# Recurrence of a two-layer kernel: one run of 128x64 score products for both inner steps, TensorE's program without its loop, and the outputs' turn placed behind the states' turns

## The chip, the cores and the metric

One core of a Trainium2 chip runs the whole program. The metric is the device time of one execution in microseconds. The kernel before takes 2533.22 us (median of 3 runs, 2533.12 to 2538.01).

## What is computed

Two adaLN layers over 16 sequences of 512 tokens with 256 channels. The attention of layer 0 is a recurrence with 16 heads of 16 dimensions: its state is two small matrices per head (4 x 16 each), updated chunk by chunk (16 tokens). Cut to what matters here:

```python
def attn(q, k, v):
    s = jnp.einsum('bqhd,bkhd->bhqk', q, k) / jnp.sqrt(jnp.asarray(q.shape[-1], q.dtype))
    p = jax.nn.softmax(s, axis=-1)
    return jnp.einsum('bhqk,bkhd->bqhd', p, v)

def step(carry, xs):
    W_in, W_out = carry
    q_t, k_t, v_t, lr_t = xs
    k_h = jax.nn.softmax(jnp.einsum('blhd,bDhd->blhD', k_t, W_in), axis=-1) * lr_t[..., 1:]
    q_h = jax.nn.softmax(jnp.einsum('blhd,bDhd->blhD', q_t, W_in), axis=-1)
    qk = jnp.einsum('bqhD,bkhD->bhqk', q_h, k_h) * mask
    o_t = jnp.einsum('bqhD,bDhd->bqhd', q_h, W_out) + jnp.einsum('bhqk,bkhd->bqhd', qk, v_t)
    W_out = W_out + jnp.einsum('bnhD,bnhd->bDhd', k_h, v_t)
    for _ in range(2):
        g_out = -attn(W_in, k_t, v_t)
        g_in = -attn(W_out, v_t, k_t)
        W_in = W_in - lr_in * g_in
        W_out = W_out - lr_out * g_out
    return ((W_in, W_out), o_t)
```

The change touches `attn(W_out, v_t, k_t)` of the two inner steps: its scores, W_out on the values of the chunk, are the "scores on the values" below.

## The kernel before

The program has three stages: projections of all 16 sequences (to about 480 us in the profile), the recurrence (481 to 1209 us), and the rest of layer 0 with layer 1 (to the end). Only the recurrence is touched.

The recurrence walks 32 chunks in order. All 16 x 16 pairs of sequence and head are done together: a state is a 128x128 tile, and for the products it lies "spread" in a 128x1024 tile, 32 blocks of 32 columns, block-diagonal by heads. The spread (`spread`, L1289 and L1848) multiplies by 0 or 1: VectorE writes the lower 64 partitions with one instruction (L1852), ScalarE the upper 64 with four (L1292). Each engine has its own program, written in the order in which it is to run; the engines meet through counting semaphores (`Steps`: `mark` raises one, `at(c, name)` is its value when step `name` of chunk c is done, `before` that of the chunk before). All five programs walk the chunks as `Fori(0, ROUNDS)` (4 rounds) around 8 chunks written out (`CPR`). As the chunk number then hangs on a register, a wait needs a register instruction ahead of it.

TensorE's order in one chunk (L871 to L944):

1. `scores` (L830) on keys and queries, marks a0 and a1, then turns of them (L884, L887, L893), and the running sums (`sums`, L846) and state terms (`add_state`, L854) of the outputs.
2. Three runs of `updates` (L841) on pb_1, pb_2, pb_kh: 32 products each (steps p1v, p2v, khv). khv closes W_out: VectorE then adds it (L1939, "wok") and the inner step's update (L1941, "wo1").
3. `turn_out` (L861, "ot"), four transposes of the normalised outputs of the chunk before, which ScalarE evicts (L1298, "oev").
4. The states' turns: transposes of w_out_k (L911, "two") and w_out_1 (L913, "tw1"), each then spread by VectorE and ScalarE ("xo", "xw").
5. `sums(3)`, then the scores on the values: two runs of 32 products of 128 rows x 32 columns x 16 tokens (L834), "b0" on st_out1 after "xo", "b1" on st_out2 after "xw".
6. Softmax of each in turn: VectorE takes the maxima (L1954) and subtracts them (L1956), ScalarE takes exp (L1360, "eb0", "eb1"), TensorE turns it (L925, L928), both spread it ("xb0", "xb1"), and between these stands half of `add_state((2, 3), ..)`.
7. `updates` on the keys (L841, "pb0"), the other half of `add_state((2, 3), ..)`, `updates` "pb1", then the turns of the new W_in (L937 "ti1", L942 "ti"), whose spreads start the next chunk.

```python
mm = pe.matmul(dst[j * NST:(j + 1) * NST, x], by_tile(st)[:, j, x], tok[:, j, x], start=True, stop=True)
```

On VectorE the order after "bs1" is: osum (row sums of the outputs, L1865), xb0, omean (L1869), xb1. GpSimd's "oc" (L1570) waits for omean.

Of the kernel before, what the change touches and what calls it, by code (L numbers as in the profile page):

```python
# [6 lines left out]
P = 128  # L7
# [13 lines left out]
ROUNDS = CHUNKS // CPR  # L21
# [51 lines left out]
def adaln_two_layers(nc, x, w_in, taps, w_out, ln_g, ln_b, w_in_init, w_out_init, u1, v1, b1, u2, v2, b2,  # L73
                     cond, wmod, w_attn, w_proj, w_r, w_k, w_v, mu, ident_c, blocks_c, parity_c, mask_c, four_c, scan_c, out):
    ctx = ExitStack()
    with ctx:
# [95 lines left out]
        st_in1, st_in2, st_out1, st_out2 = (carve(TILES * NST) for _ in range(4))  # L172
# [19 lines left out]
        m_b, rl_i = carve(2, GG), carve(2, PP)  # L192
# [60 lines left out]
        def hold(eng):  # L253
# [43 lines left out]
            "bm0", "bs0", "bm1", "bs1", "osum", "xb0", "omean", "xb1", "irec0", "ilr0", "imul0", "wi1", "irec1", "ilr1", "imul1", "wi", "xs", "xi"])  # L297
# [3 lines left out]
                                       "eb0", "eb1", "xb0", "xb1", "rv3", "rv2", "xs", "xi"])  # L301
        re_pe = Steps(sem("re_pe"), ["a0", "a1", "traw", "te1", "te2", "r01", "p1v", "p2v", "khv", "ot", "two", "tw1", "sm3", "b0", "b1",
                                     "tb0", "tb1", "pb0", "r23", "pb1", "ti1", "ti"])
# [405 lines left out]
        def _(pe):  # L709
# [126 lines left out]

            def updates(dst, pb, rows, js):

                for x in range(PP):
                    for j in js:  # L840
                        mm = pe.matmul(dst[j * NST:(j + 1) * NST, x], by_tile(pb)[:, j, x], rows[:, j * PP + x], start=True, stop=True)  # L841
                return mm
# [71 lines left out]

# [1325 lines left out]
```

## Time and profile before

| | |
|---|---|
| median of 3 runs | 2533.22 us |
| the profiled execution, its own time | 2533.14 us |
| its span | 2531.3 us |
| recurrence, 32 chunks | 481 to 1209 us, 22.75 us each |
| busy over the span | TensorE 86%, VectorE 63%, ScalarE 62%, GpSimd 43% |
| granted TensorE clock, whole span | 0.93 |

Times in the profile are microseconds from the start of the span; a line number is that of the listing above. "PE" is TensorE's matmuls, "PEld" its weight loads, DVE VectorE, ACT ScalarE, POOL GpSimd. "idle before ... <- X" tells what ended the idle time; "issue" means that nothing which the profile shows was waited for.

### The profile page before, as it was taken

To read this page: it belongs to the slowest core of one execution; us is meant where nothing else is said; L and a number is where in the kernel's file an instruction comes from. 1 tells how busy PE (TensorE), PEld (TensorE's weight loads), DVE (VectorE), ACT (ScalarE), POOL (GpSimd) and SP (SyncE) were. 2 spreads that over 40 slices of the span, in tenths; PEclk is the share of its full clock that TensorE was granted. 3 is DMA by queue.
4 is the path that set the end of the run, shared out by engine and by line. 5 is a ranking of instruction groups with operands and counts; after the bars stand their busy time and mean duration, and the time that the engine had idled before them with its cause. 6 is when DMAs were issued, how large, how long until landed. Compare 5 with 4: busy or idle time off the path is not lost.

```text
span 2531.3 us, 88431 instructions
## 1 busy us (share of the span) xinstructions
PE 2166.9 (86%) x32563; PEld 1390.6 (55%) x32563; DVE 1596.6 (63%) x3896; ACT 1576.2 (62%) x4079; POOL 1086.6 (43%) x1204
## 2 busy tenths in 40 slices
PE   5999997487788787787389999999999999999898
PEld 4554454255555555455246566575664756647466
DVE  1888886477666666667247477474764747647465
ACT  2788787377676666667248466484654846547464
POOL 0122122377677677667524423344233442334323
PEclk8999999699788888889699999999999999999999
DMA  4455555623233233231421231312213122130120
GB/s 150 126 158 164 162 156 160 119 68 85 66 79 74 68 85 76 56 72 39 137 52 31 71 75 43 94 32 66 67 48 94 42 58 60 52 89 4 39 50 18
DMA packets 403135, 201.57 MB, mean 80 GB/s; under 512 B 273776, under 2 KB 389104, under 8 KB 402688
## 3 DMA queue, kind: packets, MB, share of 16 engines
q1 hardware_dynamic: 402688, 195.65, 29.6%
q8 instruction: 276, 4.52, 0.8%
q14 instruction: 171, 1.40, 0.2%
HBM read 101.67 MB, written 69.27 MB: 68 GB/s over the span
## 4 chain that ended last, share of the span: by engine, by line
PE 55%; ACT 15%; issue 12%; DVE 12%; POOL 3%; DMA 1%; SPq 1%; ACTq 0%; DVEq 0%; POOLq 0%
PE psum L982 11%; PE psum L763 6%; ACT arena L1492 6%; ACT arena L1292 5%; PE psum L1075 4%; DVE arena L1785 4%; PE psum L834 3%; PE psum L846 3%; PE psum L1034 3%; PE psum L841 3%; PE psum L1042 3%; PE psum L1111 3%; PE psum L1148 2%; PE psum L1098 2%; PE psum L1129 2%
## 5 line engine op out<-in xcount | busy, mean ns | idle before, releaser
L1716 POOL TENSOR_TENSOR arena<-arena 128x400 f32<-128x400 f32 x256 | 218.3, 853 | 482.8 <-DVE arena L2132 482.8
L1292 ACT ACTIVATE arena<-psum,scan_sb 64x128 f32<-64x128 f32 x1152 | 308.3, 361 | 106.0 <-PE psum L911 88.4
L1492 ACT ACTIVATE arena<-psum,arena 128x100 f32<-128x100 f32 x1024 | 269.5, 365 | 6.0 <-DVE arena L2124 5.9
L1785 DVE SCALAR_TENSOR_TENSOR arena<-psum,taps_sb,arena 128x511 f32<-128x511 f32 (+2 forms) x288 | 213.8, 747 | 60.7 <-ACT arena L1201 53.9
L1534 POOL TENSOR_TENSOR arena<-arena 128x512 f32<-128x512 f32 x64 | 79.4, 1274 | 359.0 <-ACT arena L1227 359.0
L763 PE MATMUL psum<-arena,w_in_sb 128*128 128x512 f32 x512 | 230.0, 598 | 0.9 <-issue 0.9
L841 PE MATMUL psum<-arena 128*32 128x17 f32 x10240 | 134.9, 191 | 98.3 <-issue 65.1
L1852 DVE TENSOR_TENSOR arena<-psum,scan_sb 64x512 f32<-64x512 f32 x290 | 189.0, 673 | 7.6 <-PE psum L942 7.6
L846 PE MATMUL psum<-arena,scan_sb 128*128 128x512 f32 x264 | 186.5, 799 | 1.9 <-DVE arena L1852 1.9
L841 PEld LDWEIGHTS psum<-arena 128*32 128x32 f32 x10240 | 115.5, 117 | 123.1 <-issue 71.7
L2124 DVE TENSOR_REDUCE arena<-psum 128x4 f32<-128x400 f32 x256 | 146.4, 573 | 57.1 <-PE psum L1098 46.7
L1484 ACT ACTIVATE arena<-psum 100x512 f32<-100x512 f32 x256 | 155.7, 608 | 41.9 <-PE psum L1111 35.7
L1609 POOL TENSOR_TENSOR arena<-arena 128x512 f32<-128x512 f32 x128 | 133.6, 1065 | 93.5 <-ACT arena L1346 88.7
L1111 PE MATMUL psum<-ident,arena 128*100 128x128 f32 x1024 | 162.8, 282 | 4.5 <-ACT arena L1484 0.5
L2128 DVE TENSOR_REDUCE arena<-arena 128x4 f32<-128x400 f32 x256 | 145.6, 569 | 19.7 <-ACT arena L1492 13.6
L763 PEld LDWEIGHTS psum<-arena,w_in_sb 128*128 128x128 f32 x512 | 95.8, 192 | 110.6 <-issue 110.1
L1098 PE MATMUL psum<-arena 64*128 64x100 f32 x2048 | 156.1, 273 | 0.0
L834 PEld LDWEIGHTS psum<-arena 128*32 128x32 f32 x8192 | 89.2, 119 | 106.5 <-ACT arena L1292 77.1
L1558 POOL TENSOR_TENSOR arena<-arena 128x512 f32<-128x512 f32 x132 | 139.6, 1058 | 0.1
L1098 PEld LDWEIGHTS psum<-arena 64*128 64x128 f32 x2048 | 137.2, 190 | 0.0
L834 PE MATMUL psum<-arena 128*32 128x16 f32 (+1 forms) x8192 | 99.1, 195 | 30.1 <-issue 18.9
L1111 PEld LDWEIGHTS psum<-ident,arena 128*100 128x100 f32 x1024 | 102.9, 128 | 35.1 <-ACT arena L1484 12.9
(220 smaller groups left out, 4712.2 us busy)
## 6 DMA issues: line engine op xcount, KB each, us to landing
arena<-arena SPq DMA_DIRECT2D x144, 128.0 KB
arena<-x SPq DMA_DIRECT2D x32, 512.0 KB, 3.9
arena<-gates_d SPq DMA_DIRECT2D x112, 128.0 KB, 4.0
v_rows_d<-arena SPq DMA_DIRECT2D x64, 136.0 KB
k_rows_d<-arena SPq DMA_DIRECT2D x64, 136.0 KB
arena<-k_rows_d SPq DMA_DIRECT2D x128, 68.0 KB, 2.0
arena<-v_rows_d SPq DMA_DIRECT2D x128, 68.0 KB, 2.2
v_d<-arena SPq DMA_DIRECT2D x32, 256.0 KB, 4.3
```

The source lines that it names most:

```text
L763: mm = pe.matmul(bank[2 + j % 6][:], w_in_sb[:, k, j * P:(j + 1) * P], a_h[:, k], start=(k == 0), stop=(k == KT - 1))
L834: mm = pe.matmul(dst[j * NST:(j + 1) * NST, x], by_tile(st)[:, j, x], tok[:, j, x], start=True, stop=True)
L841: mm = pe.matmul(dst[j * NST:(j + 1) * NST, x], by_tile(pb)[:, j, x], rows[:, j * PP + x], start=True, stop=True)
L846: return pe.matmul(bank[RUN_BANKS[j]][:], causal, kv[:, j], start=True, stop=False, skip_group_check=True)
L982: mm = pe.matmul(B(s, banks[a])[:, j * DIM:(j + 1) * DIM], lhs(k, 2 * a + j), rhs(k), start=(k == 0), stop=(k == KT - 1))
L1098: mm = pe.matmul(B(s, top)[:, k * KEYS:(k + 1) * KEYS], c_qb[s][rows, k, f], c_k[s][rows, k, f], start=False, stop=True, skip_group_check= ...
L1111: mm = pe.transpose(bank[TURNED][0:KEYS, tok(u)], c_soft[s][:, f % 2, u], ident[:])
L1292: ins = act.activation(dst.rearrange("p (t x a) -> p t x a", x=PP, a=INNER)[upper, :, x], src.rearrange("p (t a) -> p t a", a=INNER)[upper ...
L1492: act.activation(c_soft[s][:, f % 2, u], sc, ACT.Exp, bias=c_max[s][:, u:u + 1]).then_inc(c_act.mark(f"exp{s}{f}u{u}"), 1)
L1716: pool.tensor_tensor(soft, soft, c_rec[s].unsqueeze(2).broadcast_to([P, 4, KEYS]), ALU.mult).then_inc(c_pool.mark(f"prob{s}{f}"), 1)
L1785: ins = dve.scalar_tensor_tensor(out=a_acc[:, t, j:TOK], in0=bank[2 + t][:, 0:TOK - j], scalar=taps_sb[:, t % KT, col:col + 1], in1=a_acc[ ...
L1852: return dve.tensor_tensor(dst.rearrange("p (t x a) -> p t x a", x=PP, a=INNER)[rows, :, xs], src.rearrange("p (t a) -> p t a", a=INNER)[r ...
```

## The change

Three parts, all in the recurrence.

**Scores in one run.** st_out1 and st_out2 become one tile st_outs of 2048 columns, in which the 32 columns of both states for one block lie side by side. A new `scores_out` makes 32 products of 128 rows x 64 columns x 16 tokens into bank 2; block j writes partitions 0 to 63 or 64 to 127, by j % 2. It waits for both spreads. Maxima, subtraction and exp are then one instruction each over 256 columns, the turn is two transposes behind one wait, and the two spreads read alternate columns of the turned tile. `add_state((2, 3), ..)` stands as parts (0, 1, 2) ahead of the wait for exp and part (3,) behind the turn; nothing stands between "pb0" and "pb1". On VectorE osum and omean now both stand ahead of xb0.

**TensorE's loop.** TensorE's `Fori` becomes a Python `for`: all 32 chunks are written out, and its waits are on constants. The other engines keep their loops.

**The outputs' turn.** `turn_out` moves behind the two states' turns.

```diff
-        st_in1, st_in2, st_out1, st_out2 = (carve(TILES * NST) for _ in range(4))
+        st_in1, st_in2 = (carve(TILES * NST) for _ in range(2))
+        st_outs = carve(2 * TILES * NST)
+        st_out = [st_outs.rearrange("p (t x w a) -> p w t x a", x=PP, w=2, a=INNER)[:, w] for w in range(2)]
+        b_turned = [bank[1][:, 2 * P:4 * P].rearrange("p (t w a) -> p w t a", w=2, a=INNER)[:, w] for w in range(2)]
...
+            def scores_out(dst, tok):
+
+                to = dst.rearrange("p (h x n) -> p h x n", h=JJ // 2, n=CHUNK)
+                pairs = st_outs.rearrange("p (j x n) -> p j x n", j=JJ, n=2 * NST)
+                for x in range(GG):
+                    for j in range(JJ):
+                        rows = slice(j % 2 * 2 * NST, (j % 2 + 1) * 2 * NST)
+                        mm = pe.matmul(to[rows, j // 2, x], pairs[:, j, x], tok[:, j, x], start=True, stop=True)
+                return mm
...
-            with pe.Fori(0, ROUNDS) as n:
+            for n in range(ROUNDS):
...
-                    pe.wait_ge(pool.sem, pool.at(c, "on"))
-                    pe.wait_ge(act.sem, act.before(c, "oev"))
-                    turn_out().then_inc(mine.mark("ot"), 1)
                     pe.wait_ge(dve.sem, dve.at(c, "wok"))
                     pe.transpose(bank[3][:, 3 * P:4 * P], w_out_k, ident[:]).then_inc(mine.mark("two"), 1)
                     pe.wait_ge(dve.sem, dve.at(c, "wo1"))
                     pe.transpose(bank[0][:, 2 * P:3 * P], w_out_1, ident[:]).then_inc(mine.mark("tw1"), 1)
-
+                    pe.wait_ge(pool.sem, pool.at(c, "on"))
+                    pe.wait_ge(act.sem, act.before(c, "oev"))
+                    turn_out().then_inc(mine.mark("ot"), 1)
                     pe.wait_ge(act.sem, act.at(c, "rv0"))
                     pe.wait_ge(pool.sem, pool.before(c, "kv3"))
                     sums(3).then_inc(mine.mark("sm3"), 1)
-                    pe.wait_ge(dve.sem, dve.at(c, "xo"))
-                    pe.wait_ge(act.sem, act.at(c, "xo"))
-                    scores(grid(bank[2][:, 2 * P:3 * P], CHUNK), st_out1, v_blk[buf][:, :, :, now], every).then_inc(mine.mark("b0"), 1)
                     pe.wait_ge(dve.sem, dve.at(c, "xw"))
                     pe.wait_ge(act.sem, act.at(c, "xw"))
-                    scores(grid(bank[1][:, 2 * P:3 * P], CHUNK), st_out2, v_blk[buf][:, :, :, now], every).then_inc(mine.mark("b1"), 1)
-                    pe.wait_ge(act.sem, act.at(c, "eb0"))
-                    pe.transpose(bank[2][:, 3 * P:4 * P], e_b[:, 0], ident[:]).then_inc(mine.mark("tb0"), 1)
-                    add_state((2, 3), before_last, (0, 1))
-                    pe.wait_ge(act.sem, act.at(c, "eb1"))
-                    pe.transpose(bank[1][:, 3 * P:4 * P], e_b[:, 1], ident[:]).then_inc(mine.mark("tb1"), 1)
+                    scores_out(bank[2][:, 2 * P:4 * P], v_blk[buf][:, :, :, now]).then_inc(mine.mark("b"), 1)
+                    add_state((2, 3), before_last, (0, 1, 2))
+                    pe.wait_ge(act.sem, act.at(c, "eb"))
+                    for h in range(2):
+                        mm = pe.transpose(bank[1][:, (2 + h) * P:(3 + h) * P], e_b[:, h], ident[:])
+                    mm.then_inc(mine.mark("tb"), 1)
+                    add_state((2, 3), before_last, (3,)).then_inc(mine.mark("r23"), 1)
                     pe.wait_ge(dve.sem, dve.at(c, "xb0"))
                     pe.wait_ge(act.sem, act.at(c, "xb0"))
                     updates(grid(bank[3][:, 0:PP * ROW17], ROW17), pb_in[0], k_rows[i % 2], every).then_inc(mine.mark("pb0"), 1)
-                    add_state((2, 3), before_last, (2, 3)).then_inc(mine.mark("r23"), 1)
...
+                    dve.wait_ge(pe.sem, pe.at(c, "b"))
+                    dve.tensor_reduce(m_b, b_now, AX.X, ALU.max).then_inc(mine.mark("bm"), 1)
+                    dve.wait_ge(mine.sem, mine.at(c, "bm"))
+                    dve.tensor_tensor(e_b.rearrange("p h (x m) -> p (h x) m", m=CHUNK), b_now, over(m_b, CHUNK), ALU.subtract).then_inc(mine.mark("bs"), 1)
```

TensorE's program before, in the second of the eight chunks of a round, from the third run of updates to `sums(3)` (L841 updates, L861 outputs' turn, L911 and L913 states' turns, L846 sums; REGISTER_ALU and ISA stand for waits):

```order
L841 MATMUL psum<-arena 32x17 x32
L907 ISA
L908 REGISTER_ALU
L861 MATMUL psum<-ident,arena 128x128 x4
L910 REGISTER_ALU
L911 MATMUL psum<-ident,arena 128x128
L912 REGISTER_ALU
L913 MATMUL psum<-ident,arena 128x128
L915 REGISTER_ALU
L916 REGISTER_ALU
L846 MATMUL psum<-arena,scan_sb 128x512
```

The same place in the changed program, where L855 are all three runs of updates, L922 and L924 the states' turns, L875 the outputs' turn and L860 the sums:

```order
L855 MATMUL psum<-arena 32x17 x96
L922 MATMUL psum<-ident,arena 128x128
L924 MATMUL psum<-ident,arena 128x128
L875 MATMUL psum<-ident,arena 128x128 x4
L860 MATMUL psum<-arena,scan_sb 128x512
```

The four output transposes went behind the two state transposes, and no instruction of its own stands for a wait any more.

The next stretch before, from the first scores on the values to the first updates on the keys (L834 scores, L925 and L928 turns of exp, L854 `add_state`, L841 updates):

```order
L834 MATMUL psum<-arena 32x16 x32
L921 REGISTER_ALU
L922 REGISTER_ALU
L834 MATMUL psum<-arena 32x16 x32
L924 REGISTER_ALU
L925 MATMUL psum<-ident,arena 128x128
L854 MATMUL psum<-arena,scan_sb 128x8x16 x4
L927 REGISTER_ALU
L928 MATMUL psum<-ident,arena 128x128
L929 REGISTER_ALU
L930 REGISTER_ALU
L841 MATMUL psum<-arena 32x17 x32
```

The same stretch in the changed program (L848 `scores_out`, L868 `add_state`, L937 the turn, L855 both runs of updates):

```order
L848 MATMUL psum<-arena 64x16 x32
L868 MATMUL psum<-arena,scan_sb 128x8x16 x6
L937 MATMUL psum<-ident,arena 128x128 x2
L868 MATMUL psum<-arena,scan_sb 128x8x16 x2
L855 MATMUL psum<-arena 32x17 x64
```

Two runs of 32 became one with 64 output partitions each, and all the state terms now stand ahead of the updates.

## Rows read from the trace of the kernel before

**Rows 1.** Busy time by engine, clock and DMA in the recurrence and in one chunk

```profile
core 0: us, PE busy (x) PEld busy (x) DVE busy (x) ACT busy (x) POOL busy (x), PEclk, DMA share, GB/s
481.00:1209.00 728.00, 577.70 (x20173) 386.60 (x20174) 488.12 (x1440) 489.51 (x1636) 509.77 (x604) 0.87 0.30 69
568.70:589.00 20.30, 16.16 (x630) 10.86 (x630) 15.20 (x46) 15.03 (x51) 16.29 (x20) 1.00 0.31 71
```

**Rows 2.** Waits, 481 to 1209 us: who waited for whom, total, times, longest

```profile
ACT arena L1292 <- PE psum L911: 88.4, 32, 4.1
...
PE psum L841 <- issue: 65.1, 40, 2.5
...
DVE arena L1939 <- PE psum L841: 40.8, 28, 2.1
```

**Rows 3.** Timeline of a chunk at full clock: start, length, engine, line

```profile
573.46 0.76 PE L841 MATMUL psum<-arena 128*32 128x17 f32 x64
...
575.30 0.36 PE L841 MATMUL psum<-arena 128*32 128x17 f32 x18 [0.17 <-ACT arena L1292]
577.39 0.58 PE L841 MATMUL psum<-arena 128*32 128x17 f32 x46 [1.73 <-issue]
577.95 0.65 PE L861 MATMUL psum<-ident,arena 128*128 128x128 f32 x4
...
578.02 0.29 DVE L1939 TENSOR_TENSOR arena<-arena,psum 128x128 f32<-128x128 f32 x1 [1.29 <-PE psum L841]
...
578.44 0.27 PE L911 MATMUL psum<-ident,arena 128*128 128x128 f32 x1
```

**Rows 4.** DMA queue of the instructions, 481 to 1209 us: packets, MB, share

```profile
q8 instruction: 166, 2.72, 1.7%
```

**Rows 5.** The same chunk, from the states' spreads to those of the softmax

```profile
578.75 2.14 ACT L1292 ACTIVATE arena<-psum,scan_sb 64x128 f32<-64x128 f32 x8 [2.23 <-PE psum L911]
...
580.11 1.88 PE L834 MATMUL psum<-arena 128*32 128x16 f32 x128
...
583.03 2.14 ACT L1292 ACTIVATE arena<-psum,scan_sb 64x128 f32<-64x128 f32 x8
```

**Rows 6.** Timeline of a chunk partly at half clock, matmuls and weight loads

```profile
784.02 0.29 PE L911 MATMUL psum<-ident,arena 128*128 128x128 f32 x1
784.48 2.07 PE L846 MATMUL psum<-arena,scan_sb 128*128 128x512 f32 x2
786.48 1.76 PE L834 MATMUL psum<-arena 128*32 128x16 f32 x128
...
788.87 0.52 PEld L854 LDWEIGHTS psum<-arena,scan_sb 32*128 32x128 f32 x8
791.28 0.93 PEld L854 LDWEIGHTS psum<-arena,scan_sb 32*128 32x128 f32 x8
```

**Rows 7.** Groups by line, weight loads of three widths: busy, mean ns, idle before

```profile
L834 PEld LDWEIGHTS psum<-arena 128*32 128x32 f32 x8192 | 89.2, 119 | 106.5 <-ACT arena L1292 77.1 <-issue 28.4
...
L1042 PEld LDWEIGHTS psum<-arena,u_sb 128*64 128x64 f32 x224 | 13.7, 134 | 48.1 <-ACT arena L1452 42.8 <-issue 5.3
...
L1098 PEld LDWEIGHTS psum<-arena 64*128 64x128 f32 x2048 | 137.2, 190 | 0.0
```

**Rows 8.** Groups by line, instructions of 256 columns, and one pair of transposes

```profile
L1898 DVE TENSOR_REDUCE arena<-psum 128x64 f32<-128x256 f32 x32 | 13.6, 425 | 7.1 <-PE psum L884 7.1
L1901 DVE TENSOR_TENSOR arena<-psum,arena 128x256 f32<-128x256 f32 x32 | 13.3, 415 | 0.0
L1334 ACT ACTIVATE psum<-arena 128x256 f32<-128x256 f32 x32 | 12.4, 388 | 23.4 <-DVE arena L1901 23.4
...
569.98 0.44 PE L884 MATMUL psum<-ident,arena 128*128 128x128 f32 x2
```

**Rows 9.** Timeline where the second round of the loops begins

```profile
658.36 1.27 PE L834 MATMUL psum<-arena 128*32 128x32 f32 x80 [2.46 <-issue]
658.43 1.28 ACT L1311 ACT_TABLE_LOAD   x1 [2.22 <-issue]
661.50 0.84 PE L834 MATMUL psum<-arena 128*32 128x16 f32 x48 [1.88 <-issue]
```

More of the change, by code:

```diff
@@ L296, in adaln_two_layers @@
             "prec", "plr", "pmul", "xrec", "xlr", "xmul", "wo2", "wok", "wo1", "qrec", "qh", "xo", "xw",
-            "bm0", "bs0", "bm1", "bs1", "osum", "xb0", "omean", "xb1", "irec0", "ilr0", "imul0", "wi1", "irec1", "ilr1", "imul1", "wi", "xs", "xi"])
+            "bm", "bs", "osum", "omean", "xb0", "xb1", "irec0", "ilr0", "imul0", "wi1", "irec1", "ilr1", "imul1", "wi", "xs", "xi"])
         out_names = lambda js: [f"{n}{j}" for j in js for n in ("mul", "sa", "sb")]
@@ L300, in adaln_two_layers @@
         re_act = Steps(sem("re_act"), ["rawk", "rawq", "oln", "e1", "orstd", "ek", "e2", "x1", "x2", "xk", "khc", "rv0", "rv1", "xo", "xw", "oev",
[L301 to L303 removed]
+                                       "eb", "xb0", "xb1", "rv3", "rv2", "xs", "xi"])
+        re_pe = Steps(sem("re_pe"), ["a0", "a1", "traw", "te1", "te2", "r01", "p1v", "p2v", "khv", "two", "tw1", "ot", "sm3", "b", "tb", "r23", "pb0", "pb1", "ti1", "ti"])
         RUN_BANKS = (6, 7, 5, 6)
@@ L1357, in _ @@
                     out_cols(past // CPB, past % CPB).then_inc(mine.mark("oev"), 1)
+                    act.wait_ge(dve.sem, dve.at(c, "bs"))
+                    act.activation(e_b, e_b, ACT.Exp, scale=attn).then_inc(mine.mark("eb"), 1)
+                    act.wait_ge(pe.sem, pe.at(c, "tb"))
                     for r in range(2):
-                        act.wait_ge(dve.sem, dve.at(c, f"bs{r}"))
-                        act.activation(e_b[:, r], e_b[:, r], ACT.Exp, scale=attn).then_inc(mine.mark(f"eb{r}"), 1)
-                    for r, b in enumerate((2, 1)):
-                        act.wait_ge(pe.sem, pe.at(c, f"tb{r}"))
-                        spread(pb_in[r], bank[b][:, 3 * P:4 * P]).then_inc(mine.mark(f"xb{r}"), 1)
+                        spread(wide(pb_in[r]), b_turned[r]).then_inc(mine.mark(f"xb{r}"), 1)
                     evict(3)
@@ L1366, in _ @@
                     act.wait_ge(pe.sem, pe.at(c, "ti1"))
-                    spread(st_in1, bank[2][:, 0:P]).then_inc(mine.mark("xs"), 1)
+                    spread(wide(st_in1), thin(bank[2][:, 0:P])).then_inc(mine.mark("xs"), 1)
                     act.wait_ge(pe.sem, pe.at(c, "ti"))
-                    spread(st_in2, bank[1][:, 0:P]).then_inc(mine.mark("xi"), 1)
+                    spread(wide(st_in2), thin(bank[1][:, 0:P])).then_inc(mine.mark("xi"), 1)
             def finish(e):
@@ L1851, in spread @@
                 shape = [P // 2, TILES, PP // 2, INNER]
-                return dve.tensor_tensor(dst.rearrange("p (t x a) -> p t x a", x=PP, a=INNER)[rows, :, xs],
-                                         src.rearrange("p (t a) -> p t a", a=INNER)[rows].unsqueeze(2).broadcast_to(shape),
+                return dve.tensor_tensor(dst[rows, :, xs], src[rows].unsqueeze(2).broadcast_to(shape),
                                          mask8[rows, xs].unsqueeze(1).unsqueeze(3).broadcast_to(shape), ALU.mult)
@@ L1857, in _ @@
             for h in range(2):
-                spread(st_in2, bank[3][:, 3 * P:4 * P], h).then_inc(st_dve.mark(f"x{h}"), 1)
+                spread(wide(st_in2), thin(bank[3][:, 3 * P:4 * P]), h).then_inc(st_dve.mark(f"x{h}"), 1)
             dve.wait_ge(st_dve.sem, st_dve.at(0, "x1"))
@@ L1882, in _ @@
                 p_inv, x_inv = (bank[m][:, PP * ROW17:PP * ROW17 + PP] for m in (0, 2))
-                b_now = [eights(bank[m][:, 2 * P:3 * P], CHUNK) for m in (2, 1)]
+                b_now = eights(bank[2][:, 2 * P:4 * P], CHUNK)
                 m_a = bank[3][:, 2 * P:2 * P + GG]
@@ L1910, in _ @@
                     dve.wait_ge(pe.sem, pe.at(c, "te1"))
-                    spread(pb_1, bank[0][:, 3 * P:4 * P]).then_inc(mine.mark("x1"), 1)
+                    spread(wide(pb_1), thin(bank[0][:, 3 * P:4 * P])).then_inc(mine.mark("x1"), 1)
                     dve.wait_ge(mine.sem, mine.at(c, "krec"))
@@ L1917, in _ @@
                     dve.wait_ge(pe.sem, pe.at(c, "te2"))
-                    spread(pb_2, bank[2][:, 2 * P:3 * P]).then_inc(mine.mark("x2"), 1)
+                    spread(wide(pb_2), thin(bank[2][:, 2 * P:3 * P])).then_inc(mine.mark("x2"), 1)
                     dve.wait_ge(mine.sem, mine.at(c, "kh"))
-                    spread(pb_kh, kh_new).then_inc(mine.mark("xk"), 1)
+                    spread(wide(pb_kh), thin(kh_new)).then_inc(mine.mark("xk"), 1)
                     dve.wait_ge(pe.sem, pe.at(c, "p1v"))
@@ L1974, in _ @@
                     dve.wait_ge(pe.sem, pe.at(c, "ti1"))
-                    spread(st_in1, bank[2][:, 0:P]).then_inc(mine.mark("xs"), 1)
+                    spread(wide(st_in1), thin(bank[2][:, 0:P])).then_inc(mine.mark("xs"), 1)
                     dve.wait_ge(pe.sem, pe.at(c, "ti"))
-                    spread(st_in2, bank[1][:, 0:P]).then_inc(mine.mark("xi"), 1)
+                    spread(wide(st_in2), thin(bank[1][:, 0:P])).then_inc(mine.mark("xi"), 1)
             dve.wait_ge(re_pool.sem, re_pool.at(CHUNKS - 1, "o2"))
```

37 lines of the change are left out of this document (16 added, 21 removed).

## The prediction

> **What bounds the kernel now.** Only the recurrence changes, so I read its stretch alone. The busy times come first [rows 1]: over its 728 us TensorE is busy 578, GpSimd 510, VectorE and ScalarE 488 and 490, so none is full, and the granted clock is 0.87, which is a mix of the 2.4 and 1.2 GHz levels. 32 chunks share the 728 us. An undisturbed one, at full clock throughout, takes 20.3 us. Four engines that are all partly idle mean a chain: what counts is how long one chunk's dependence takes to go round. The waits [rows 2] show its links. ScalarE waits 88 us for the turn of W_out, VectorE 41 us for the third run of updates, and TensorE itself stands still in the update runs for 65 us with "issue" as the reason, 40 times in 32 chunks.
>
> The timeline of one chunk shows that stop [rows 3]: the third run begins at 575.30, gets through 18 records in 0.36 us, and goes on 1.73 us later. VectorE's sum, which closes W_out, had been waiting for 1.29 us. The instructions' own DMA queue [rows 4] explains it: 166 transfers in the recurrence for 40347 matmul and load records [rows 1], so one for about 243, in pieces of 16 KB. Three update runs are 384 records and need under 3 us of work, so a whole piece is used up before the next has come. I read the stop as a late fetch of code.
>
> From there the path of a chunk is: W_out closed, outputs' turn, states' turns, eight spreads on ScalarE, scores, softmax, spreads, two update runs, W_in, next chunk.
>
> **The change part by part**, each per chunk (32 chunks) unless said otherwise. The sum is made against the profiled execution's 2533.14 us, 0.1 us below the median of the runs.
>
> *The scores.* Before, at full clock, the turn of W_out starts at 578.44 and the second score run ends at 580.11 + 1.88 = 581.99, 3.55 later [rows 3, 5]. That the first run is finished by then costs nothing: ScalarE's eight spreads take 2.14 us and the first run lies beside the last four. Now all products wait for the eighth spread, at 578.75 + 2.14 = 580.89, 2.45 behind the turn, and the whole run stands on the path. It is 32 products of two passes, 64 loads of 64 columns. No such run is in the trace, so I bound it. From below: 64 records at the pace of an update run, 0.76 us, if width is free. From above: loads cost by width. Three widths take 119, 134 and 190 ns [rows 7] (the first mean holds half-clock loads too), so about 28 ns more per 32 columns. A load of 128 columns with two tiles in turn, as here, comes every 0.52 / 8 = 65 ns at full clock and every 0.93 / 8 = 116 ns at half [rows 6]. With half the columns that is 32 and 58 ns, so the run takes 2.0 us at full and 3.7 us at half clock. I take this end, less a little for the first load (1.9), because the new products have that row's form: two tiles and wide loads. Full clock: 2.45 + 0.05 + 1.9 = 4.4 against 3.55, and 3.7 where the second run starts a bit later; I count +0.8. Half clock: before, 786.48 + 1.76 - 784.02 = 4.2 [rows 6]. Now the outputs' turn (0.65, some 1.0 at half clock) stands ahead of the sums, which take 2.07, so the run starts some 3.2 behind the turn, and 3.7 makes 6.9: +2.6. The half clock comes in short stretches; for 24 chunks at full and 8 at half in this place: 24 x 0.8 + 8 x 2.6 = **+40 us**. Lower end: 2.45 + 0.05 + 0.8 = 3.3 against 3.7, -0.4 x 32 = -13.
>
> *The softmax.* Before, the second softmax follows its scores by 583.03 - 581.99 = 1.04 us [rows 5], and the first is hidden. Now 256 columns go through at once [rows 8]: 0.42 + 0.42 + 0.39 + two transposes 0.44 + four hand-overs of 0.05 = 1.87. The turn of the second half was hidden before and is on the path now. +0.83 x 32 = **+27 us**.
>
> *State terms out of the middle, osum and omean ahead of xb0.* The second update run no longer waits for eight loads (0.52 to 0.93, rows 6), but it waits for ScalarE's next four spreads, half of 2.14 us [rows 5], so at most 0.2 us is won at full clock, and VectorE's four short steps on the first update take it up. osum and omean run beside exp and the transposes. **0**, at best -6.
>
> *The outputs' turn behind.* The outputs' turn starts at 577.95, W_out is ready at 578.02 + 0.29 = 578.31, its turn starts at 578.44 [rows 3]: 0.1 us to win here, some 0.4 where the clock is halved and the four transposes take twice as long. 0.25 x 32 = **-8 us**. Nobody waits for the outputs' turn soon enough to mind: ScalarE evicts it behind its eight spreads.
>
> *Fewer records.* A chunk has 630 + 630 matmul and load records [rows 1]; 128 go, and the register instructions of the waits with them. A piece of code then lasts longer, 4.5 instead of 5.2 fetches per chunk. As 4.5 is not near a whole number, the place where a piece ends moves from chunk to chunk, instead of staying in the third update run. I place the pieces over the chunk: a stop needs a whole piece inside the 384 dense records and the turns around them, which is so for some 60% of the positions. The stop holds VectorE up by 41 us in all [rows 2]; 40% of it is **-16 us**. Both ends: 0 and -41. The Trainium skill, "Runtime: NRT & Kernel Launch", section "Instruction fetch mechanics", says that crossing into a new block of code is mostly hidden; by that rule this term is 0 and the sum 2582. Rows 2 and 3 speak against it, since the engine stands still for nothing else, so I keep the term.
>
> *Register instructions.* Ahead of a wait in a dense run they show as up to 0.1 us (the 0.17 ahead of a run [rows 3] against 0.05 for a bare hand-over): **-3 us** in all.
>
> *The loop.* At each of the three returns TensorE stands for 2.46 us, then 1.88 us [rows 9]. The first is hidden: ScalarE has its own return and loads its table until 658.43 + 1.28 = 659.71, and the copy that the chain needs comes after. The second holds up the first turns of the chunk. -2.2 x 3 = **-7 us**.
>
> Sum: 40 + 27 + 0 - 8 - 16 - 3 - 7 = +33, so 2533 + 33 = **2566 us**.
>
> **Rivals.** *Width is free* (0.21): the run goes at the pace of the other runs. The 32-column runs keep four tiles going at 0.76 / 64 = 12 ns a pair [rows 3], near what issue alone may allow. Against it: the widths' durations. -13 + 27 - 8 - 16 - 3 - 7 = -20: 2513 us. This is the other side: it decides where a pair of the new run takes under some 16 ns.
>
> *A tile's product costs the same at both widths, and only the number of tiles halves* (0.12): 24 ns a pair by the same row, a run of 1.5 us at most, 1.3 if the pair is 20. Then 2.5 + 1.4 = 3.9 against 3.7, +0.2 x 32 = +6 in place of +40: -1, 2532 us, no change. The Trainium skill, "TensorEngine Tiling (Array Packing)", section "Theoretical Speedup", has up to 4x for 32 columns and 2x for 64, which is this case.
>
> *The half clock spreads* (0.11): a longer idle stretch around the softmax lets TensorE's clock fall in 20 chunks rather than 8 at the scores: 12 x 0.8 + 20 x 2.6 = 62 instead of 40, 2588 us. For it: 0.87 already, and more waiting per chunk. Against it: fewer stops in the updates.
>
> *All stops vanish* (0.10): -41 in place of -16: 2541 us. It needs fetches to keep up with 384 dense records, which rows 3 deny.
>
> **How the numbers follow.** The forecast's own case has 0.46, with 2550 to 2582 as its range. 0.2% (5 us) is about what a measurement of this kernel tells from no change, so 2528 to 2538 is "same". Slower: 0.46 + 0.11 + 0.10, less a little for its lower edge, 0.65. Same: 0.12. Faster: 0.21 and the lower edge of the second rival, 0.23. The range takes in all but the ends: 2512 to 2600.
>
> **What would show it.** Right: the run of 64-column products takes 1.8 to 2.0 us at full clock, 30 ns a pair; from its end to the first spread is 1.9 us; "issue" idle in the updates falls to some 60% of its 65 us; a fetch for about 250 records, some 145 in all; after each return the second stop is gone; an undisturbed chunk takes 21 to 22 us. Wrong: a run under 1.0 us, or undisturbed chunks under 20 us; or the waits of VectorE for the third update run gone entirely. If the clock in the recurrence moves by more than 0.03 from 0.87, that term was missing or too small.

## The result, and the profile after

| | before | after |
|---|---|---|
| time, median of 4 runs | 2534.12 us | 2616.86 us (2608.39 to 2621.16) |
| ratio, 95% interval | | 1.0319 [1.0289, 1.035] |
| profiled run: span; recurrence | 2531.3; 728 us | 2612.3; 809 us |

The kernel is 83 us slower where +33 was forecast, and outside the range. All of it is in the recurrence. Busy time and clock there, the columns as in [rows 1]:

```profile
481.00:1290.00 809.00, 652.91 (x18112) 453.43 (x18112) 481.66 (x1375) 485.17 (x1600) 512.62 (x606) 0.75 0.27 61
```

The other engines work as long as before. TensorE has a tenth fewer records and is busy 75 us longer. Some 27 us of it are the new run's own (it is busy 82 us, the two old runs were 55); the rest came with the clock, which fell from 0.87 to 0.75. With two levels, a mean of c puts 2 x (1 - c) of the stretch at 1.2 GHz: 189 us before, 404 us now. The waits, against [rows 2], and the instructions' queue, against [rows 4]:

```profile
DVE arena L1960 <- PE psum L848: 114.4, 32, 4.7
...
ACT arena L1368 <- DVE arena L1962: 105.9, 32, 4.4
ACT arena L1302 <- PE psum L922: 70.2, 32, 4.0
...
PE psum L855 <- issue: 40.1, 22, 2.9
...
DVE arena L1946 <- PE psum L855: 22.4, 16, 1.9
```

```profile
q8 instruction: 143, 2.34, 1.2%
```

The first two are the new chain: VectorE waits 3.6 us a chunk for the scores, ScalarE 3.3 us for the softmax. TensorE's stops in the updates ("issue") fell from 65.1 to 40.1 us and VectorE's wait for them from 40.8 to 22.4, with 143 fetches: as forecast. A chunk's middle where the run has the full clock (columns as in [rows 3]):

```profile
568.94 0.94 PE L860 MATMUL psum<-arena,scan_sb 128*128 128x512 f32 x1
...
569.82 2.04 PE L848 MATMUL psum<-arena 128*64 128x16 f32 x64
...
571.91 0.42 DVE L1960 TENSOR_REDUCE arena<-psum 128x16 f32<-128x256 f32 x1 [3.04 <-PE psum L848]
572.37 0.42 DVE L1962 TENSOR_TENSOR arena<-psum,arena 128x256 f32<-128x256 f32 x1
...
572.83 0.42 ACT L1368 ACTIVATE arena<-arena 128x256 f32<-128x256 f32 x1 [2.72 <-DVE arena L1962]
...
573.30 0.69 PE L937 MATMUL psum<-ident,arena 128*128 128x128 f32 x2 [0.57 <-ACT arena L1368]
...
574.02 2.15 ACT L1302 ACTIVATE arena<-psum,scan_sb 64x128 f32<-64x128 f32 x8 [0.78 <-PE psum L937]
...
575.29 2.08 PE L855 MATMUL psum<-arena 128*32 128x17 f32 x128 [0.58 <-DVE arena L1860]
```

The run takes 2.04 us. From its end (571.86) to the first spread there are 2.16 us. The granted clock is at its lower level from 573.0 on: two transposes take 0.69 instead of 0.44, and the 128 update pairs 2.08 instead of 2 x 0.76 [rows 3]. The same place with the clock halved earlier:

```profile
867.62 0.48 PE L922 MATMUL psum<-ident,arena 128*128 128x128 f32 x1 [0.38 <-DVE arena L1946]
...
868.21 1.06 PE L875 MATMUL psum<-ident,arena 128*128 128x128 f32 x4
869.06 1.92 PE L860 MATMUL psum<-arena,scan_sb 128*128 128x512 f32 x2
870.91 3.60 PE L848 MATMUL psum<-arena 128*64 128x16 f32 x64
```

Here the turn of W_out and the end of the run are 6.89 us apart, against 4.2 in [rows 6]. I read the same marks off all chunks' timelines (means of the first 31, us a chunk). A chunk begins with its first scores, on the keys and queries; "W_out closed" is the end of VectorE's sum, "scores" goes from the start of the first to the end of the last run on the values, and the last turn is that of the new W_in:

| | W_out closed | to its turn | to the scores | scores | to the 1st update | to the 2nd | 2nd update | to last turn | to next chunk | sum |
|---|---|---|---|---|---|---|---|---|---|---|
| before | 10.22 | 0.25 | 2.16 | 1.94 | 2.22 | 1.60 | 0.97 | 1.48 | 1.92 | 22.8 |
| after | 9.97 | 0.06 | 3.18 | 2.54 | 3.38 | 1.02 | 1.10 | 2.27 | 1.73 | 25.3 |

The clock is at its lower level when the scores begin in 20 of 31 chunks (before: 14) and when the second update begins in all 31 (before: 11). It often changes within a stretch. The chunks in which it stayed at one level, with their mean:

| | full clock throughout | lower clock throughout | changes |
|---|---|---|---|
| scores, before | 17: 1.89 | 2: 1.91 | 12 |
| scores, after | 11: 2.04 | 8: 3.60 | 12 |
| turn of W_out to the scores' end, before | 7: 4.11 | 2: 4.18 | 22 |
| the same, after | 4: 4.70 | 8: 6.89 | 19 |
| first update to the last turn, before | 18: 3.39 | 0 | 13 |
| the same, after | 0 | 30: 4.41 | 1 |

### The profile page after: what moved, and what is told of

Same layout as the page of the kernel before. It is cut to its first block, busy times and chain, and to the rows that moved or that the text cites. A ratio compares the mean times of both kernels' runs of the same rounds, so it can differ in the third digit from the quotient of the medians.

```text
span 2612.3 us, 83282 instructions
## 1 busy us (share of the span) xinstructions
PE 2246.2 (86%) x30515; PEld 1458.6 (56%) x30515; DVE 1590.6 (61%) x3832; ACT 1573.7 (60%) x4047; POOL 1089.1 (42%) x1204
## 3 DMA queue, kind: packets, MB, share of 16 engines
q8 instruction: 247, 4.05, 0.7%
## 4 chain that ended last, share of the span: by engine, by line
PE 54%; DVE 16%; issue 12%; ACT 12%; DMA 1%; POOL 1%; SPq 1%; DVEq 1%; ACTq 0%; POOLq 0%
PE psum L992 11%; ACT arena L1500 7%; PE psum L767 6%; PE psum L1085 4%; PE psum L860 4%; DVE arena L1793 4%; PE psum L848 3%; PE psum L1044 3%; PE psum L1052 3%; PE psum L855 2%; PE psum L1158 2%; PE psum L1024 2%; PE psum L1121 2%; PE psum L838 1%; DVE arena L1860 1%
## 5 line engine op out<-in xcount | busy, mean ns | idle before, releaser
L1860 DVE TENSOR_TENSOR arena<-psum,scan_sb 64x512 f32<-64x512 f32 x290 | 188.5, 675 | 40.8 <-PE psum L952 28.9
L855 PE MATMUL psum<-arena 128*32 128x17 f32 x10240 | 143.8, 200 | 70.4 <-issue 40.1
L860 PE MATMUL psum<-arena,scan_sb 128*128 128x512 f32 x264 | 201.3, 859 | 2.7 <-DVE arena L1860 1.9
L855 PEld LDWEIGHTS psum<-arena 128*32 128x32 f32 x10240 | 131.1, 132 | 89.8 <-issue 43.1
L992 PE MATMUL psum<-arena 128*128 128x256 f32 x512 | 115.1, 381 | 3.6 <-DVE arena L2146 3.6
L1024 PE MATMUL psum<-mask_sb,identb 128*128 128x400 bf16 x518 | 113.9, 345 | 0.0
```

The lines of the kernel that those rows point to most:

```text
L860: return pe.matmul(bank[RUN_BANKS[j]][:], causal, kv[:, j], start=True, stop=False, skip_group_check=True)
L992: mm = pe.matmul(B(s, banks[a])[:, j * DIM:(j + 1) * DIM], lhs(k, 2 * a + j), rhs(k), start=(k == 0), stop=(k == KT - 1))
L1024: pe.matmul(spare[:, 0:2 * KT * KEYS], identb[:], mask_sb[:, 0:2].rearrange("p a b -> p (a b)"), start=True, stop=True)
L1860: return dve.tensor_tensor(dst[rows, :, xs], src[rows].unsqueeze(2).broadcast_to(shape), mask8[rows, xs].unsqueeze(1).unsqueeze(3).broadca ...
```

## The experiments

Ratios are to the kernel before on the same chip, with 95% intervals; a point is 1% of its time. Medians of different kernels may come from different chips, so differences between them are best taken from the ratios.

**Undoing one part of the change.** First TensorE's loop back, then the 32-column products back:

```diff
-            for n in range(ROUNDS):
+            with pe.Fori(0, ROUNDS) as n:
```

> The changed kernel with TensorE's loop put back. If writing it out saved what I counted (2.2 us at each of three returns, 0.1 us of register work a chunk, some stops): 10 to 25 us slower than the changed kernel, 2627 to 2642. Rival: the register instructions and returns were hidden, within 5 us of 2616.

2622.64 us, 1.031 [1.0268, 1.0351]: writing out the program makes no difference to the changed kernel.

```diff
-                    for j in range(JJ):
-                        rows = slice(j % 2 * 2 * NST, (j % 2 + 1) * 2 * NST)
-                        mm = pe.matmul(to[rows, j // 2, x], pairs[:, j, x], tok[:, j, x], start=True, stop=True)
+                    for h in range(JJ // 2):
+                        for q in range(JJ):
+                            j, part = 2 * h + q // 2, slice(q % 2 * NST, (q % 2 + 1) * NST)
+                            mm = pe.matmul(to[q * NST:(q + 1) * NST, h, x], pairs[:, j, x, part], tok[:, j, x], start=True, stop=True)
```

> The changed kernel with each 64-column product of the merged run made as two of 32 columns into the same places; all else as changed. Theory of width (wide loads are the price): the run returns to 64 pairs x 2 at 9 ns (full) or 13 ns (half clock), 1.2 to 1.8 us instead of 2.0 to 3.6, and -0.8 to -1.8 us a chunk: 2616 becomes 2560 to 2590. Theory of the clock (the idle stretch of the merged softmax lets the granted clock fall, and the half clock is the price): the run is again four tiles wide, but the clock in the recurrence stays near 0.75 and the updates on the keys stay at half clock, so at most 30 us come back. Theory of code fetches: 128 more records a chunk bring back stops, and it is no faster than 2610.

2632.75 us, 1.037 [1.0329, 1.0411]. I took this to say that width costs nothing. That was wrong: a later run with the same products shows it. This one has 128 more records a chunk than the changed kernel, and TensorE now stops in the merged run itself:

```profile
PE psum L849 <- issue: 20.8, 12, 2.5
```

Ten of its 31 merged runs take 3.2 to 4.4 us, the others 1.26 to 1.9. With all stops it stands still for 110 us in the recurrence, the changed kernel for 51.

**One part alone, in the kernel before.** The loop written out; the outputs' turn behind the states' turns; the merged scores and softmax.

> The kernel before with TensorE's loop alone written out. Same theory: -10 us from the returns and register work, and as 33 fewer records a chunk hardly move where a piece of code ends (4.9 fetches instead of 5.1), the stop in the third update run stays: 2518 to 2528. Rival: within 5 us of before. Rival of the fetches: the stops wander and 20 to 40 us are won.

2583.71 us, 1.0151 [1.0106, 1.0197]. Not a gain but the first surprise. The stops in the updates are fewer (46.4 us), those in the scores more (42.2 instead of 18.9), and the clock is 0.80.

> The kernel before with the outputs' turn moved behind the states' turns, nothing else. As predicted: 0.25 us a chunk gained, 8 us or 0.3%, ratio 0.995 to 0.999; the wait of ScalarE for the turn of W_out shrinks by that. Rival: the turn now stands between W_out's turns and the sums, which delays the score runs by 0.6 us a chunk where ScalarE isn't the later one: ratio 1.003 to 1.008.

2546.14 us, 1.0075 [1.0048, 1.0102]. The turn of W_out begins 0.19 us sooner, but the scores 0.73 us later behind it (2.89 instead of 2.16), since the outputs' turn and then the sums of 0.9 to 2 us stand between. The rival holds.

> The kernel before with the merged scores and softmax alone: TensorE's loop kept, the outputs' turn still ahead of W_out's. Theory A (the 64-wide run and the one softmax lengthen each chunk, and the longer idle stretch behind them pulls the clock down): nearly the whole loss is in this part, ratio 1.025 to 1.035, clock in the recurrence 0.77 or less, half clock over 330 us. Rival B (the order behind the outputs' turn is what costs in the changed kernel): ratio under 1.015.

2615.32 us, 1.0342 [1.0302, 1.0381], clock 0.75. The merge alone has the whole loss.

**Where the pieces of code end.** Products that nobody reads, in the first chunk of each round, move what follows against the ends of the pieces. A chunk of the kernel before has 1297 records on average, the waits' own included, so 166 fetches in 32 chunks make some 250 records a piece. It is taken as 256 here, which the run with exactly 256 more records bears out:

```diff
+                    if i == 0:
+                        pe.wait_ge(act.sem, act.before(c, "oev"))
+                        for _ in range(64):
+                            pe.matmul(bank[4][0:NST, 0:CHUNK], identb[:, 0:NST], mask_sb[:, 0, 0:CHUNK], start=True, stop=True)
                     for t, name in enumerate(("rawk", "rawq")):
```

> The kernel before with 64 tiny products (128 records, about 0.8 us) in the first chunk of each round, in TensorE's idle time ahead of the first copy: every later piece of code in the round ends half a piece earlier in the work. Theory (it matters where in the chunk the pieces end, which is why writing out the loop cost 1.5%): ratio 1.008 to 1.02, issue stops leave the third update run for others. Rival (a stop comes wherever the dense part outruns the fetches, whatever the piece's position): ratio 0.999 to 1.002, and the cost of writing out the loop has another cause.

2590.88 us, 1.0256 [1.0222, 1.029]. The place matters, and by more than the theory's 2 points.

With `range(128)`:

> Control for the kernel whose first chunks had 64 tiny products (1.026): the same place and the same wait, but 128 products, 256 records, which is one whole piece of code. Position theory: the pieces end where they end in the kernel before, so only the products' own 4 x 1.6 us are left: ratio 1.000 to 1.006, half clock near 191 us. Rival (the products or their wait do the harm, by themselves): at least as bad as 64 of them, ratio 1.025 or more.

2539.98 us, 1.0054 [1.0031, 1.0077].

With `range(16)`:

> The same with 16 products (32 records), so the pieces end an eighth of a piece earlier. By the lengths of the chunks in the kernel before and in the one with 64 products, placed by their position (0 to 119 records past the start there, 128 to 247 here), positions 34 to 145 are the short ones: mean chunk 22.0 to 22.6 us against 22.8, ratio 0.990 to 1.000. Rival (the time goes up with any displacement): 1.005 to 1.015.

2516.16 us, 0.9958 [0.9936, 0.998]: faster than before with more work. Mean length of a chunk by its number in the round, us:

| products | 1st | 2nd | 3rd | 4th | 5th | 6th | 7th | 8th |
|---|---|---|---|---|---|---|---|---|
| 0 | 25.9 | 22.9 | 21.8 | 21.8 | 21.1 | 22.5 | 21.4 | 25.2 |
| 128 | 29.9 | 22.9 | 21.6 | 21.6 | 21.4 | 22.3 | 21.0 | 25.2 |
| 64 | 24.3 | 21.3 | 26.3 | 24.0 | 23.8 | 24.1 | 26.0 | 26.6 |
| 16 | 24.7 | 20.9 | 20.7 | 22.1 | 22.1 | 21.6 | 22.4 | 24.2 |

A whole piece of added records gives the same row within 0.4 us but for its own 4 us in the first chunk; half a piece changes nearly all others. So the place of the pieces is worth up to 5 us a chunk, and the kernel before stands well. The waits of TensorE with 64 products show the stops where they cost more, in the score runs (18.9 us there before):

```profile
PE psum L834 <- issue: 48.3, 31, 2.4
PE psum L841 <- issue: 33.8, 33, 2.4
```

In sum the stops hardly grew, 90 us against 84, for a loss of 64 us. What did grow is the time at the lower clock: 0.81 over 783 us makes 298 us, against 189. The place of the stops and the clock moved together here, and no run parts them.

**The clock.** 28 products of 128 columns a chunk into an unused bank, in the waits of the changed kernel for W_out, exp and the spreads (8, 6 and 14):

```diff
+            def keep_busy(times, step):
+
+                pe.wait_ge(re_act.sem, step)
+                for _ in range(times):
+                    pe.matmul(bank[4][:, 0:P], identb[:], mask_sb[:, 0, 0:P], start=True, stop=True)
+
...
+                    keep_busy(8, act.before(c, "oev"))
                     pe.wait_ge(dve.sem, dve.at(c, "wok"))
...
+                    keep_busy(6, act.at(c, "oev"))
                     pe.wait_ge(act.sem, act.at(c, "eb"))
...
+                    keep_busy(14, act.at(c, "oev"))
                     pe.wait_ge(dve.sem, dve.at(c, "xb0"))
```

> The changed kernel with small dummy products on TensorE (bf16, 128x128, into the free bank 4) where it idles: 8 ahead of the wait for W_out, 6 ahead of the wait for exp, 14 ahead of the wait for the softmax's spreads. Theory of the clock: the granted clock in the recurrence rises from 0.75 towards 0.9 or more and the time falls by 30 to 60 us, to 2555 to 2590, although TensorE does more. Theory of width or of the longer chain alone: the clock rises and the time changes by less than 10 us, or it grows where the dummies get in the way.

2574.52 us, 1.0131 [1.0087, 1.0176]:

```profile
481.00:1249.00 768.00, 627.15 (x19008) 455.61 (x19008) 480.25 (x1374) 481.43 (x1599) 510.94 (x605) 0.89 0.28 65
```

The clock is back at 0.89, and half the loss is gone (by the ratios 1.9 of 3.2 points): the score run takes 2.11 us on average instead of 2.54, and the way from the first update to the last turn 3.36 instead of 4.39. The 56 more records a chunk also move the pieces, but the stops in the updates stayed what they were, 40.1 us, and W_out is closed 0.42 us later, so the gain isn't theirs:

```profile
PE psum L855 <- issue: 40.1, 24, 2.8
```

The same in the kernel before, without the first eight:

> The kernel before with 20 idle 128x128 products a chunk (6 ahead of the wait for the first exp, 14 ahead of the wait for the first spread), all else as it was. Clock theory: half clock in the recurrence falls from 191 us to under 100 and the time by 0.3 to 1.0% (ratio 0.990 to 0.997). Rival (the clock is already high enough here, the products only stand in the way): 1.000 to 1.010.

2573.97 us, 1.0184 [1.0152, 1.0217], clock 0.88: neither case of the expectation. The time at the lower clock is 180 us, not under 100. Of the 0.67 us a chunk that were lost, 0.41 lie between the scores and the first update, where all 20 products stand; but 40 more records a chunk move the pieces too (the chunks' mean lengths by number now run from 20.9 to 28.0 us), and the two aren't parted. It says nothing of what the clock is worth.

**The merge with the pieces held.** The kernel with the merge alone, and 65 tiny products behind the run, so that a chunk has its 1297 records again:

```diff
+                    pe.wait_ge(act.sem, act.at(c, "oev"))
+                    for _ in range(65):
+                        pe.matmul(bank[4][0:NST, 0:CHUNK], identb[:, 0:NST], mask_sb[:, 0, 0:CHUNK], start=True, stop=True)
```

> Merged scores and softmax with TensorE's loop and the outputs' turn ahead, and behind the merged run 65 tiny products (130 records, 0.8 us, in the softmax's time), so that a chunk has as many records as before and each piece of code ends where it did. Position theory: what is left is the longer chain, 1.3 us for the run and the softmax by the segments, less what the clock gets back: ratio 1.010 to 1.025 against 1.034 without the padding. Rival (the lost time is the merged run's own, whatever the pieces do): 1.033 or more.

2679.78 us, 1.0614 [1.0572, 1.0656].

With `range(57)`, and 32 more in each round's first chunk:

> As the padded one, but 57 products a chunk, which makes a chunk 1280 records, five whole pieces, and 32 products (64 records) in the first chunk of each round: every chunk then stands where the fifth of a round stood in the kernel before, which was the shortest (21.1 us). Position theory: better than the padded one by 0.5% or more. Rival (positions matter little once the run is merged): the same within 0.3%.

2674.25 us, 1.0593 [1.0557, 1.0629]. Both are spoilt by the padding: in one tile it is not 0.8 us, but makes the way from the scores to the first update 5.2 and 5.0 us instead of 3.3. The two are 0.2 points apart, as the rival has it: in this form the place made no clear difference. So the padding is dealt over four tiles:

```diff
+                        pe.matmul(bank[4][q % JJ * NST:(q % JJ + 1) * NST, 0:CHUNK], identb[:, 0:NST], mask_sb[:, 0, 0:CHUNK], start=True, stop=True)
```

> The merged run of 64-column products, loop and outputs' turn as before, with 65 padding products dealt over four tiles, so that they take about 0.8 us instead of the 2 to 3.5 us that they took in one tile, and fit beside the softmax. Position theory: ratio 1.012 to 1.025, from the run to the first update at most 3.4 us. Rival (the merged form loses wherever the pieces end): 1.03 or more.

2629.59 us, 1.0396 [1.037, 1.0422]. The way to the first update is 3.97 us, 0.68 more than without padding; 22 us of the 99 (2629.59 - 2530.43) are the padding's, and 1.031 is left, as far as that way is its whole price. The rival holds: the 64-column form lost at least 3 points in every place that was tried. The same merge with 32-column products needs no padding: it has 3 records a chunk fewer than the kernel before (its edit is the one shown for 32 columns):

> Both steps' scores together and one softmax, but by the 32-column products of before, with TensorE's loop and the outputs' turn ahead: a chunk has within a few records as many as before, so the pieces of code end where they did. Position theory: what is left is the chain's own price, by the segments 0.4 us for the run behind the eighth spread and 0.8 to 1.1 us for the one softmax, 40 to 50 us in all, ratio 1.012 to 1.022. Rival (the idle stretch of the one softmax brings the clock down whatever the pieces do): 1.03 or more, with half clock over 300 us.

2561.07 us, 1.0113 [1.0091, 1.0134]. Its run at full clock:

```profile
804.99 1.27 PE L849 MATMUL psum<-arena 128*32 128x16 f32 x128 [0.72 <-ACT arena L1303]
806.19 0.94 PE L869 MATMUL psum<-arena,scan_sb 32*128 32x128 f32 x12
```

128 pairs of weight load and matmul take 1.27 us, 10 ns each; the changed kernel's 64 pairs take 2.04, 32 ns each. At the lower clock it is 1.9 to 2.1 against 3.60. So one softmax and one run for both steps cost 1.1 points, some 30 us, with the pieces nearly held, and the 64 columns add 2.0 to 2.3 points, 49 to 58 us (1.031 with the pieces held, 1.0342 without, less 1.0113). Whether the wider loads or the two tiles instead of four make the pair dearer isn't parted. The clock fell here too, to 0.80 (306 us at the lower level), so the one softmax lowers it by itself, at a small price. The shares of the 64 columns and of the clock overlap: the wide run is also what costs most at the lower clock.

**Holding the place.** The kernel before with its loop written out has 1273 records a chunk; 3 or 4 tiny products, two records each, make it 1280 on average:

```diff
+                    pe.wait_ge(act.sem, act.before(c, "oev"))
+                    for q in range((4 - i % 2) + (37 if c == 0 else 0)):
+                        pe.matmul(bank[4][q % JJ * NST:(q % JJ + 1) * NST, 0:CHUNK], identb[:, 0:NST], mask_sb[:, 0, 0:CHUNK], start=True, stop=True)
```

> The kernel before with TensorE's loop written out (1.015 so far) and padding over four tiles: 41 products in the first chunk, then 3 or 4 a chunk, so that a chunk has 1280 records, five whole pieces, and all 32 chunks stand where the 27th stood in the written-out kernel (21.7 us). Position theory: every chunk takes 21 to 22.5 us, ratio 0.975 to 0.995. Rival (the written-out form is slow in itself): 1.01 or more.

2509.02 us, 0.991 [0.989, 0.9929].

With 55 instead of 37:

> The same with 59 products in the first chunk: all chunks stand 36 records further on, where the 22nd stood in the written-out kernel (22.6 us). Position theory: the lengths of the chunks are as even as in the other, at another level; ratio 0.98 to 1.01, and the two differ by more than 0.5%. Rival: no difference between the two.

2542.51 us, 1.0047 [1.0029, 1.0064].

With 46:

> Held as the other two, 50 products in the first chunk: 18 records behind the place of the kernel with 0.991 and as far ahead of the one with 1.005. Position theory, if the dependence is smooth: 0.992 to 1.003. If a border lies between (the stop delays W_out in the one and not in the other): at one of the two ends, 0.990 or 1.005. Rival, chance differences between builds: outside 0.985 to 1.01.

2520.52 us, 0.9948 [0.9929, 0.9967]. The first takes 9.94 us to W_out, this one 10.14, the second 10.72: the place between the two gives a time between theirs, and the theory's first case holds. In the first the stops are in the updates alone (55 us, against 0.3 us in the scores), and its ratio is 2.4 points under that of the written-out kernel whose pieces drift. Here too the clock goes along: 0.88, 0.86 and 0.82 from the first to the slowest. Last, the 3 or 4 products made useful:

```diff
+                    pe.wait_ge(act.sem, act.at(c, "oev"))
+                    for q in range(2):
+                        pe.matmul(bank[4][:, 0:2 * KT * KEYS], identb[:], mask_sb[:, 0:2].rearrange("p a b -> p (a b)"), start=True, stop=True)
                     pe.wait_ge(act.sem, act.at(c, "eb0"))
```

> The held kernel of 0.991 with its 3 or 4 tiny products a chunk replaced by as many of 400 columns, 2 ahead of the wait for the first exp and 1 or 2 ahead of the wait for the first spread: same number of records, so the same places (within 7 records). Clock theory: half clock under 120 us instead of 169, and 5 to 15 us less than the held one, ratio 0.985 to 0.990. Rival (the products stand in the way, the clock is not what costs here): 0.992 to 1.000.

**2489.83 us, 0.9832 [0.9799, 0.9865]**, the fastest of all, 5% under the changed kernel. The held kernel of 0.991 and this one:

```profile
481.00:1184.00 703.00, 563.46 (x20306) 378.74 (x20306) 485.84 (x1438) 487.88 (x1630) 508.87 (x602) 0.88 0.31 71
481.00:1170.00 689.00, 559.69 (x20327) 371.17 (x20325) 486.16 (x1441) 490.99 (x1640) 513.97 (x609) 0.93 0.31 72
```

The place is that of the 0.991 kernel within 7 records, the number of records is the same, and the stops are too (56.1 us in the updates, 55.3 there); the clock went from 0.88 to 0.93 and the time down by 19 us. The products now stand in the softmax's waits and not at the chunk's start. The marks put the gain where the clock changed: to the first update the two kernels agree within 0.1 us, and from there to the next chunk it is 5.02 us instead of 5.79, with the second update at the lower clock in none of 31 chunks instead of 12. It is the clock, as far as these marks can tell.

## Why the prediction was wrong

- **The clock.** This is the failing step: the sum lets the lower clock cost something only at the scores, "for 24 chunks at full and 8 at half in this place", and prices the softmax and the updates from rows at full clock. In the changed kernel the lower clock covers the way from the first update to the last turn in 30 of 31 chunks, at 4.41 us against 3.39 at full clock, and half the recurrence in all (404 of 809 us). Two of the prediction's own signs say so: the clock moved by 0.12 from 0.87, where 0.03 was named, and no chunk took 21 to 22 us, the shortest 23.2. With most of it given back, 42 us of the 83 went. The rival "the half clock spreads" has the right count at the start of the scores (20 of 31), but the run stays at that clock in only 8 of them, and it too priced nothing behind the scores. The count was an estimate; all chunks of the trace before would have given it (14 at the scores, 11 at the second update).
- **The scores, +40.** Run: 1.9 forecast at full clock and 3.7 at half, measured 2.04 and 3.60; from the turn of W_out to its end 4.4 and 6.9 forecast, 4.70 and 6.89 measured. In all that way grew from 4.10 to 5.72 us, 52 us instead of 40; in the kernel with the merge alone to 5.25, 37 us. The mechanism holds. "Width is free" (under 16 ns a pair) is refuted, and so is "a tile's product costs the same at both widths" (24 ns, 1.5 us at most): 32 ns a pair is 3.2 times the 10 ns of the 32-column run, not twice. The three widths of [rows 7] differ by 24 ns per 32 columns on average; the 28 in the text is the step between the last two alone, and the sum doesn't use it.
- **The softmax, +27.** The way from the run to the first update grew by 1.16 (2.22 to 3.38): 37 us. Where the whole way is at full clock it takes 3.17, at the lower clock 3.51. With 32-column products it grew by 0.92.
- **State terms, osum, omean: 0.** From the first update to the last turn a chunk takes 4.39 us instead of 4.05: 11 us. The second run does need less waiting, and by more than the 0.2 us allowed (1.02 instead of 1.60); the lower clock takes it back and more, for with the clock at 0.89 the same way is 3.36.
- **The outputs' turn, -8.** Wrong in sign: by itself +19 us. The step took "0.1 us to win here, some 0.4" at the turn of W_out, and let the delay behind it count only where the clock is halved. In the merged form it cost nothing clear: the changed kernel with its loop back differs from the merge alone in this move only, its scores begin 0.49 us later behind the turn, and the two are at 1.031 and 1.0342, with intervals that overlap.
- **Fewer records, -16.** The stops fell to 62% of theirs ("some 60%") and VectorE's wait by 18 us, but W_out is closed only 0.25 us earlier, 8 us. "All stops vanish" is refuted: 51 us of stops are left. What the step also lacked is that the kernel before had its pieces in a good place. That matters for the loop's term:
- **Register instructions and the loop, -3 and -7.** Writing out the loop costs the kernel before 40 us and the changed one nothing: the gain at the returns is there (the first chunk of a round takes 23.3 us in the held kernel of 0.991, 25.9 before), but without the loop the pieces drift over all places. The Trainium skill, "Runtime: NRT & Kernel Launch", section "Instruction fetch mechanics", has crossings mostly hidden. By number that is so here: of 166 fetches, 60 show as stops in the updates and scores. But those 60 are 84 us, and half a piece more moved the time by 2.6%, so for a run of dense small products the measurement stands against it.

The sum of the terms on the path was 33; measured by marks it is 2.48 x 32 = 79. Of the missing 46 us, 12 are in the scores, 10 in the softmax, 11 in the updates, 8 in W_out and some 6 in the small gains (outputs' turn, register instructions, loop), to rounding. What stays open: why the clock falls in just these chunks, how much of the price of a misplaced piece is the clock's, and why the 64-column kernel is nearly indifferent to the place of its pieces while the 32-column one lost 2.6 points (1.0113 to 1.037) with the loop written out and the outputs' turn moved; these two were not tried apart on it.

## What to carry to other kernels

Merge two runs of small products only if the merged one keeps 32 columns and all four tiles of TensorE going: 64 pairs of 64 columns over two tiles took 1.6 times as long as 128 pairs of 32 over four. Price a longer chain at both clocks and count the chunks at each before summing. Where dense small products stop for code, measure the kernel displaced by half a piece and by a whole one before believing in a change of 2%, and use records that have to be there anyway to keep TensorE at work in its waits.

## What the runs showed of the hardware

- What the stops cost depends on where the 256-record pieces end: the second to seventh chunk of a round took 20.7 to 26.3 us for the same work, repeatably by their number in the round, and adding exactly a piece restored the pattern. The clock differed along with it (0.81 to 0.87).
- Tiny bf16 products in a single tile are slow: 65 of them added 1.9 us to the way to the first update, 30 ns each, the same over four tiles 0.7, 10 ns each.
- 28 more products a chunk made a kernel 42 us faster, with the granted clock from 0.75 to 0.89; 3 or 4 of 400 columns in place of tiny ones 19 us, from 0.88 to 0.93.
